# Moving the operands of a matmul stream to other SBUF addresses: a layernorm + S4 convolution + LoRA feed-forward kernel

## The chip, the cores and the metric

The kernel runs on one core of one Trainium2 chip, in one launch. The metric is the device time of an execution in microseconds (us). Before the change it is 442.14 us, the median of three executions (441.92 to 442.59).

## What is computed

x has 2048 rows of 512 channels. With xn the layernorm of each row:

```
s = causal convolution of xn along its 512 channels with an S4 kernel K, plus D * xn
ffn(xn) = W2' (silu(W1' xn) * (W3' xn))   hidden width 1376, each W' = W + 2 * B A (LoRA, rank 16)
out = x + s * silu(ffn(xn))
```

K comes from the S4 parameters (64 states) by a Cauchy sum and an inverse transform of length 512. All inputs are float32.

## The kernel before

**Tiling.** The rows are worked on in four blocks of 512 rows. Channels lie on the 128 partitions, in four chunks c of 128; the 512 rows of a block are the free dimension of every large matmul. The hidden width is cut into 11 tiles j (ten of 128, the last of 96). For a tile, TensorE computes the gate product (w1, bank h1), the up product (w3, bank h3), and the down product (w2, banks f0 to f3) of the tile before it. At the end of a block the S4 convolution is ten 128-square products of a Toeplitz tile `tzs` with the rows.

**Precision.** Each operand is held as two parts, high and low, in the type fp32r. `three` (lines 776 to 780) issues three matmuls for a product: low stationary with high moving (line 778), high with low (779), high with high (780). Each is a load of the stationary operand (LDWEIGHTS, 128 columns of 4 bytes) and a MATMUL that streams 512 columns of 4 bytes. So a gate, an up and a down product of one tile are 12 matmuls each, called a run below, and a block is 33 runs and 30 matmuls of convolution, 426 in all.

**Order.** The instructions are placed by hand. The block loop on TensorE is, for each tile, gate (12), up (12), down of the tile before (12); the last down tile alternates with the convolution, chunks 3 to 0. ScalarE does silu and the high part of the product, VectorE the multiplication and the low part; the normalized rows of the next block are made beside. The first block also folds the LoRA product into each weight tile as it comes from memory (small matmuls of lines 760 and 765 into two spare banks, then line 611, 493 and 621), and works out the S4 kernel on GpSimd. From then on the weights stay in SBUF.

**The layout.** Every partition holds the same byte map. `put` places a tensor at the next multiple of 32 bytes. Before the change the map starts with w13 (the folded w1 and w3), then w2f (the folded w2), xt (the split rows: two blocks, two parts, four chunks of 2048 bytes), the LoRA stack (over which `xres`, `gate` and others lie later), xn, g, ghl (the split product g: two parts of 2048 bytes), tz, tzs and small things. Scratch tensors of the first block lie inside regions that are filled later: `lora_first`, `lora_spread`, `lora_spread_split` and `rows_1` in w13, the S4 temporaries in w2f from tile 5, the raw weights in the second half of xt.

**Weight groups.** Tiles 0, 1 and 2 of w13 are groups by themselves; 3 and 4, 5 and 6, 7 and 8, 9 and 10 are pairs, kept by chunk, part and kind. A chunk of a single group is 512 bytes, of a pair 1024, of the last pair (128 + 96 columns) 896. `w13_tile` (line 331) gives the stationary operand of a product.

**Residues.** Taken modulo 2048 bytes and from the start of the map, in the kernel before: xt, all of w2f and the groups of w13 up to tile 8 start at 0, the up weights of the last pair at 1024, ghl and tzs at 128.

Of the kernel before, what the change touches and what calls it, by code (L numbers as in the profile page):

```python
# [28 lines left out]
F32R = mybir.dt.float32r  # L29

P = 128
D = 512
HID = 1376
R = 16
# [3 lines left out]
BLK = 512  # L38
NBLK = ROWS // BLK
RT = BLK // P  # L40
DC = D // P
HT = (HID + P - 1) // P
# [7 lines left out]
def hs(j):  # L50

    return min(P, HID - j * P)
# [7 lines left out]
def group(t):  # L60

    if t < PAIRED_FROM:
        return t, hs(t)
    t0 = t - (t - PAIRED_FROM) % 2
    return t0, hs(t0) + hs(t0 + 1)
# [7 lines left out]
def part_chunks(t):  # L73

    if t < PAIRED_FROM:
        return range(DC)
    h = t - group(t)[0]
    return range(h * DC // 2, (h + 1) * DC // 2)


def part_cols(t):
    return len(part_chunks(t)) * group(t)[1]


PART_AT = [sum(part_cols(u) for u in range(t)) for t in range(HT)]


# [8 lines left out]
LORA_FIRST = 3 * D + 5 * P  # L96
LANES_ST, LANES_MV = ST_COLS * R // P, MV_COLS * R // P
# [101 lines left out]
def build(nc, x, xT, w1, w3, w2, lora, lora_st, lora_mv, s4_lanes, s4_vc, s4_bp, s4_scalars, trig, lanes, dft, outT):  # L199
    ctx = ExitStack()  # L200
    with ctx:
        base = (nc.sbuf_base + 63) // 64 * 64

        def at(name, shape, off, dt=F32):
            return nc.alloc_sbuf_tensor_at(name, shape, dt, offset=base + off)


        top = [0]

        def put(name, shape, dt=F32):  # L210

            off = (top[0] + 31) // 32 * 32
            top[0] = off + int(np.prod(shape[1:])) * 4
            return at(name, shape, off, dt)

        w13 = put("w13", [P, 4 * DC * HID], F32R)
        w2f_off = top[0]
        w2f = put("w2f", [P, HT, 2, D], F32R)
        xt_off = top[0]
        xt = put("xt", [P, 2, 2, DC, BLK], F32R)  # L220
        lora_off = top[0]
        lst = put("lora_stack", [len(STACK) * R, LORA_COLS], F32R)
        xn_off = top[0]
        xn = put("xn", [P, RT, D])
        g = put("g", [P, BLK])
        ghl = put("ghl", [P, 2, BLK], F32R)
        tz = put("tz", [P, D])
        tzs = put("tzs", [P, 2, D], F32R)
        lane_c = put("lane_c", [P, EYE + P])
# [16 lines left out]

        raw = at("raw", [P, 6, BLK], xt_off + 2 * DC * BLK * 4)

        lr = at("lora_first", [R, LORA_FIRST], 7 * 4 * DC * P * 4)
        spread = at("lora_spread", [P, LANES_ST + LANES_MV], 4 * 4 * DC * P * 4)  # L250
        spread_hl = at("lora_spread_split", [P, 2, LANES_ST + LANES_MV], 5 * 4 * DC * P * 4, F32R)

        s4_tile = 5
        top[0] = w2f_off + s4_tile * 2 * D * 4
        trig_sb = put("trig_sb", [P, 2, D])
        den_re = put("den_re", [P, D])
        den_im = put("den_im", [P, D])
# [3 lines left out]
        even_odd = put("even_odd", [P, 2, D // 2])  # L261
        vc_sb = put("vc_sb", [NS, 2 * P])
        krow = put("krow", [P, P + D])
        assert top[0] <= w2f_off + HT * 2 * D * 4


        xres = at("xres", [P, 2, (xn_off - lora_off) // 4], lora_off)
        gate = at("gate", [P, 2, BLK], lora_off + DC * BLK * 4)
        rows_next = at("rows_next", [P, 2, D], lora_off + (DC + 2) * BLK * 4)
        scale_rows = at("scale_rows", [P, 2, BLK], lora_off + (DC + 4) * BLK * 4)  # L270
        assert lora_off + (DC + 6) * BLK * 4 <= xn_off

        rows_tile = 9
        rows_1 = at("rows_1", [P, RT, D], rows_tile * 4 * DC * P * 4)

        k_dram = nc.dram_tensor("k_scratch", [P, P + D], F32, kind="Internal")
        scales_dram = nc.dram_tensor("scales_scratch", [2, BLK], F32, kind="Internal")
# [2 lines left out]
        def bank(name):  # L280
            return ctx.enter_context(nc.psum_tensor(name, [P, BLK], F32))
# [3 lines left out]
        f = [bank(f"f{i}") for i in range(DC)]  # L285
# [45 lines left out]
        def w13_tile(kind, j, hl):  # L331

            t0, units = group(j)
            n = DC * units
            s = 4 * DC * P * t0 + ((kind // 2) * 2 + hl) * n
            u = (j - t0) * P
            return w13[:, s:s + n].rearrange("p (c u) -> p c u", c=DC)[:, :, u:u + hs(j)]

        def folded(kind, j, hl):

            if kind == 2:
                return w2f[0:hs(j), j, hl, :]
            t0, units = group(j)
            s = 4 * DC * P * t0 + ((kind // 2) * 2 + hl) * DC * units + part_chunks(j)[0] * units
            return w13[:, s:s + part_cols(j)]

        def raw_slot(kind, j):
# [2 lines left out]
        def raw_tile(kind, j):  # L350

            s = raw_slot(kind, j)
            return raw[0:hs(j), s, :] if kind == 2 else raw[:, s, 0:part_cols(j)]
# [10 lines left out]

        def resid(par, c):

            return xres[:, par, c * BLK:(c + 1) * BLK]

        def row_tile(b, r):

# [19 lines left out]
        def _(sync):  # L390
# [26 lines left out]
                sync.dma_start(raw_tile(kind, j), src).then_inc(raw_in[raw_slot(kind, j)], 16)  # L417

            def load_residual(b, par):
                dst = xres[:, par, 0:DC * BLK].rearrange("p (c r) -> p c r", c=DC)  # L420
                src = xT[:, :, bass.ds(b * BLK, BLK)]
                sync.dma_start(dst, src).then_inc(res0_in if isinstance(b, int) and b == 0 else res_in, 16)

            def store(b, par):
                for n, c in enumerate(OUT_ORDER):
                    sync.wait_ge(res_done, b * DC + n + 1)
                    sync.dma_start(outT[c * P:(c + 1) * P, bass.ds(b * BLK, BLK)], resid(par, c)).then_inc(out_done, 16)
# [60 lines left out]
        def _(act):  # L488
            def fold_hi(kind, j):
                act.wait_ge(fold_added, FOLD_NO[kind, j] + 1)  # L490
                if (kind, j) == (1, rows_tile):
                    act.wait_ge(stats_done, 2 * RT)
                nc.scalar.copy(folded(kind, j, 0), raw_tile(kind, j)).then_inc(whi_done, 1)  # L493
# [110 lines left out]
        def _(dve):  # L604
# [12 lines left out]
            def fold_lo(kind, j):  # L617
                if (kind, j) in POOL_LO:
                    return
                dve.wait_ge(whi_done, FOLD_NO[kind, j] + 1)  # L620
                nc.vector.tensor_tensor(folded(kind, j, 1), raw_tile(kind, j), folded(kind, j, 0).bitcast(F32),  # L621
                                        ALU.subtract).then_inc(wlo_done, 1)
# [42 lines left out]
            def out_sum(b, par):  # L665
                for n, c in enumerate(OUT_ORDER):
                    e = b * DC + n
                    dve.wait_ge(gate_done, e + 1)
                    dve.wait_ge(conv_ready, e + 1)
                    nc.vector.tensor_tensor(gate[:, n % 2, :], gate[:, n % 2, :], conv[c][:, :], ALU.mult) \  # L670
                        .then_inc(conv_used, 1)
                    dve.wait_ge(conv_used, e + 1)
                    if c < 2:
                        dve.sem_inc(spare_free[c], 1)
                    wait_residual(dve, b)
                    nc.vector.tensor_tensor(resid(par, c), resid(par, c), gate[:, n % 2, :], ALU.add) \
                        .then_inc(res_done, 1)
# [66 lines left out]
        def _(pe):  # L744
# [31 lines left out]
            def three(out, w, m, start, stop):  # L776

                pe.matmul(out, w[1], m[0], start=start, stop=False)  # L778
                pe.matmul(out, w[0], m[1], start=False, stop=False)  # L779
                return pe.matmul(out, w[0], m[0], start=False, stop=stop)  # L780

            def hidden(b, par, j, kind, out, rows=slice(0, BLK)):
                for c in range(DC):
                    if j == 0 and kind == 1 and not (isinstance(b, int) and b == 0):
                        pe.wait_ge(xlo_done, b * DC + c + 1)
                    mm = three(out[0:hs(j), rows], [w13_tile(kind, j, hl)[:, c, :] for hl in (0, 1)],
                               [xt[:, par, hl, c, rows] for hl in (0, 1)], c == 0, c == DC - 1)
                return mm
# [7 lines left out]
            def start():  # L796
# [16 lines left out]
                for c in range(DC):  # L813
                    pe.matmul(h1[:, lo], w13_tile(1, 0, 0)[:, c, :], xt[:, 0, 0, c, lo], start=(c == 0), stop=False)
                wait_split(pe, 1, 0)
                pe.wait_ge(xlo_done, RT // 2)
                for c in range(DC):
                    pe.matmul(h1[:, lo], w13_tile(1, 0, 1)[:, c, :], xt[:, 0, 0, c, lo], start=False, stop=False)
                    pe.matmul(h1[:, lo], w13_tile(1, 0, 0)[:, c, :], xt[:, 0, 1, c, lo], start=False, stop=(c == DC - 1))
# [21 lines left out]
                    pe.wait_ge(gate_done, b * DC)  # L841

            def down_chunk(j, c):
                return three(f[c][:, :], [w2f[0:hs(j), j, hl, c * P:(c + 1) * P] for hl in (0, 1)],
                             [ghl[0:hs(j), hl, :] for hl in (0, 1)], j == 0, j == HT - 1)

            def down(b, j):
# [88 lines left out]
        def _(pool):  # L936
# [28 lines left out]
            def next_scale(b, par):  # L965

                pool.wait_ge(scale_rows_in, 16 * b)
                pool.wait_ge(res_in, 16 * b)
                for c in range(DC):
                    tt(xnt[:, par, 1, c, :], resid(par, c), scale_rows[:, 0, :], ALU.mult).then_inc(scaled, 1)  # L970
# [5 lines left out]
            def fold_lo(kind, j):  # L976
                pool.wait_ge(whi_done, FOLD_NO[kind, j] + 1)
                tt(folded(kind, j, 1), raw_tile(kind, j), folded(kind, j, 0).bitcast(F32), ALU.subtract) \
                    .then_inc(wlo_pool, 1)
                pool.wait_ge(wlo_pool, POOL_LO.index((kind, j)) + 1)  # L980
# [157 lines left out]
```

## Time and profile before

| | |
|---|---|
| median of three executions | 442.14 us |
| span of the profiled execution | 439.7 us |
| TensorE matmul busy | 429.8 us, 98% of the span, 1868 matmuls |
| TensorE weight load busy | 341.6 us, 78% |
| VectorE, ScalarE, GpSimd busy | 159.6, 100.2, 63.6 us |
| DMA | 26.19 MB, mean 60 GB/s |

The span runs from the first to the last instruction of the profiled execution. Matmuls are pipelined: each is listed with about 0.39 us, but they start some 0.23 us apart, and it is the distance of the starts that makes the time. The matmul of the next product may have its stationary operand loaded while the one before streams (engine PEld beside PE).

### The profile page before, as it was taken

How to read it: one execution, taken by the hardware profiler on the slowest of the kernel's cores; microseconds unless marked ns; L12 is line 12 of the kernel's file. 1: busy time of each engine (PE TensorE's matmuls, PEld its weight loads, DVE VectorE, ACT ScalarE, POOL GpSimd, SP SyncE). 2: the span in 40 equal slices, each digit the busy share in tenths (PEclk: the TensorE clock that was granted, in tenths of full speed). 3: DMA queues.
4: the chain of work that ended last, by engine and by line, in shares of the span. 5: the costliest groups of instructions: out<-in, count | busy, mean ns of one | idle time of the engine just before them, and what ended most of it. 6: DMA issues, size and time to landing. Idle time of an engine off the chain costs nothing.

```text
span 439.7 us, 5019 instructions
## 1 busy us (share of the span) xinstructions
PE 429.8 (98%) x1868; PEld 341.6 (78%) x1868; DVE 159.6 (36%) x245; ACT 100.2 (23%) x167; POOL 63.6 (14%) x127
## 2 busy tenths in 40 slices
PE   8979999999999999999999999999999999999995
PEld 8857777776777888888878888888878888888774
DVE  3537665554539432122224232132224211111114
ACT  3433332232223111122112111122112111111111
POOL 1326541621222011400000011400000000000000
PEclk9989999999999999999999999999999999999998
DMA  8493643222040610100001510100002000000002
GB/s 267 114 197 104 220 144 97 66 70 75 18 133 37 215 49 0 48 1 0 1 0 72 167 48 0 48 0 0 0 0 86 10 0 0 0 0 0 0 0 95
DMA packets 14063, 26.19 MB, mean 60 GB/s; under 512 B 2480, under 2 KB 4208, under 8 KB 14032
## 3 DMA queue, kind: packets, MB, share of 16 engines
q1 hardware_dynamic: 13888, 25.41, 19.3%
q0 software_dynamic: 160, 0.59, 0.4%
q8 instruction: 8, 0.13, 0.1%
q14 instruction: 7, 0.06, 0.1%
HBM read 20.37 MB, written 4.53 MB: 57 GB/s over the span
## 4 chain that ended last, share of the span: by engine, by line
PE 92%; DMA 3%; SPq 1%; DVE 1%; ACT 1%; POOL 1%; issue 1%; DVEq 0%
PE h L778 20%; PE h L779 19%; PE h L780 19%; PE f L778 10%; PE f L780 9%; PE f L779 9%; DMA lora_stack<-lora_spread_split 2%; PE spare L765 2%; DMA xn<-x_dram 1%; PE spare L760 1%; SPq L457 1%; PE spare L780 1%; PE spare L778 1%; PE spare L779 1%; PE spare L884 0%
## 5 line engine op out<-in xcount | busy, mean ns | idle before, releaser
L778 PE MATMUL h<-xt,w 128*128 (+4 forms) x356 | 140.5, 395 | 0.6 <-DVE w L621 0.6
L779 PE MATMUL h<-xt,w 128*128 (+4 forms) x356 | 138.2, 388 | 0.0
L780 PE MATMUL h<-xt,w 128*128 (+4 forms) x356 | 138.1, 388 | 0.0
L778 PEld LDWEIGHTS h<-xt,w 128*128 128x128 f32 (+1 forms) x356 | 66.4, 186 | 18.4 <-issue 1.8
L657 DVE TENSOR_TENSOR g<-g,h 128x512 f32<-128x512 f32 (+1 forms) x44 | 30.2, 687 | 132.7 <-PE h L780 132.7
L780 PEld LDWEIGHTS h<-xt,w 128*128 128x128 f32 (+1 forms) x356 | 66.3, 186 | 15.0
L779 PEld LDWEIGHTS h<-xt,w 128*128 128x128 f32 (+1 forms) x356 | 66.3, 186 | 14.2
L662 DVE TENSOR_TENSOR ghl<-g,ghl 128x512 fp32r<-128x512 f32 (+1 forms) x44 | 32.7, 742 | 104.5 <-ACT ghl L519 104.4
L778 PE MATMUL f<-ghl,w2f 128*128 128x512 f32 (+1 forms) x176 | 70.3, 399 | 0.0
L780 PE MATMUL f<-ghl,w2f 128*128 128x512 f32 (+1 forms) x176 | 69.5, 395 | 0.0
L779 PE MATMUL f<-ghl,w2f 128*128 128x512 f32 (+1 forms) x176 | 69.2, 393 | 0.0
L519 ACT CAST ghl<-g 128x512 fp32r<-128x512 f32 (+1 forms) x44 | 27.3, 620 | 173.1 <-PE f L780 164.0
L778 PEld LDWEIGHTS f<-ghl,w2f 128*128 128x128 f32 (+1 forms) x176 | 33.0, 188 | 8.6 <-issue 0.3
L780 PEld LDWEIGHTS f<-ghl,w2f 128*128 128x128 f32 (+1 forms) x176 | 33.0, 188 | 7.8
L779 PEld LDWEIGHTS f<-ghl,w2f 128*128 128x128 f32 (+1 forms) x176 | 33.1, 188 | 7.5
L509 ACT ACTIVATE g<-h 128x512 f32<-128x512 f32 (+1 forms) x44 | 26.3, 598 | 54.2 <-PE h L780 53.8
L611 DVE SCALAR_TENSOR_TENSOR raw<-spare,raw 128x512 f32<-128x512 f32 (+2 forms) x33 | 22.3, 676 | 8.2 <-PE spare L765 7.1
L493 ACT CAST w<-raw 128x512 fp32r<-128x512 f32 (+1 forms) x22 | 13.4, 610 | 40.7 <-DVE raw L611 40.6
L949 POOL TENSOR_TENSOR scales<-moments,lane_c 128x2 f32<-128x2 f32 x8 | 2.3, 289 | 130.3 <-DVE moments L633 130.2
L949 POOL TENSOR_TENSOR normal_rows<-xres,scale_rows 128x512 f32 (+1 forms) x12 | 15.6, 1328 | 24.2 <-DMA scale_rows<-scales_scratch 12.2
L621 DVE TENSOR_TENSOR w<-raw,w 128x512 fp32r<-128x512 f32 (+1 forms) x18 | 14.4, 798 | 2.5 <-ACT w L493 2.4
L532 ACT ACTIVATE gate<-f 128x512 f32<-128x512 f32 x16 | 9.5, 598 | 22.2 <-PE f L780 19.6
(101 smaller groups left out, 270.8 us busy)
## 6 DMA issues: line engine op xcount, KB each, us to landing
raw<-w_dram SPq DMA_DIRECT2D x28, 256.0 KB, 3.4
xres<-xT_dram SPq DMA_DIRECT2D x4, 1024.0 KB, 7.2
outT_dram<-xres SPq DMA_DIRECT2D x16, 256.0 KB, 2.4
rows_next<-x_dram SPq DMA_DIRECT2D x4, 512.0 KB, 3.5
scale_rows<-scales_scratch SPq DMA_DIRECT2D x3, 512.0 KB, 3.8
xn<-x_dram SPq DMA_DIRECT2D x4, 256.0 KB, 4.3
rows<-x_dram SPq DMA_DIRECT2D x2, 512.0 KB, 7.1
raw<-w_dram SPq DMA_DIRECT2D x4, 224.0 KB, 2.5
```

Of the source, the lines that this page charges most:

```text
L493: nc.scalar.copy(folded(kind, j, 0), raw_tile(kind, j)).then_inc(whi_done, 1)
L509: nc.scalar.activation(g[0:hs(j), :], h1[0:hs(j), :], ACT.Silu).then_inc(silu_done, 1)
L519: nc.scalar.copy(ghl[0:hs(j), 0, :], g[0:hs(j), :]).then_inc(ghi_done, 1)
L532: nc.scalar.activation(gate[:, n % 2, :], f[c][:, :], ACT.Silu).then_inc(gate_done, 1)
L611: nc.vector.scalar_tensor_tensor(out=rt, in0=sp[bk][0:rt.shape[0], 0:fold_cols(kind, j)], scalar=LORA_SCALE, in1=rt, op0=ALU.mult, op1=ALU ...
L621: nc.vector.tensor_tensor(folded(kind, j, 1), raw_tile(kind, j), folded(kind, j, 0).bitcast(F32), ALU.subtract).then_inc(wlo_done, 1)
L657: nc.vector.tensor_tensor(g[0:hs(j), :], g[0:hs(j), :], h3[0:hs(j), :], ALU.mult).then_inc(g_done, 1)
L662: nc.vector.tensor_tensor(ghl[0:hs(j), 1, :], g[0:hs(j), :], ghl[0:hs(j), 0, :].bitcast(F32), ALU.subtract).then_inc(glo_done, 1)
L778: pe.matmul(out, w[1], m[0], start=start, stop=False)
L779: pe.matmul(out, w[0], m[1], start=False, stop=False)
L780: return pe.matmul(out, w[0], m[0], start=False, stop=stop)
L949: return nc.gpsimd.tensor_tensor(out, a, c, op)
```

## The change

The map is laid out anew; no instruction is added, removed or moved in the order of any engine.

- xt now comes first in the map (start 0), then w13, then w2f, then ghl, then the LoRA stack, xn, g and the rest.
- Each group of w13 is put at a residue modulo 2048 of its own, from a table: gate and up of tile 0 at 0 and 16, of tile 1 at 32 and 64, of tile 2 at 96 and 128, of pair 3 at 192 and 256, of pair 5 at 320 and 384, of pair 7 at 448 and 512, gate of pair 9 at 512, and its up weights right behind (1536).
- The down tiles, all in one tensor, get 0, 128, 256, 320, 384, 416, 448, 464, 480, 496 and 512 bytes of padding added up in front of them. With w2f at residue 512 their starts are at 512, 640, 768, 832, 896, 928, 960, 976, 992, 1008 and 1024; ghl behind them starts at 1024. tzs starts at 1152.
- The scratch tensors of the first block move with the tile that they lay in before. `xres` is addressed as one flat row with a computed start instead of a dimension for the two slots; the bytes are the same.

```diff
+STAGGER = {(1, 0): 0, (3, 0): 16, (1, 1): 32, (3, 1): 64, (1, 2): 96, (3, 2): 128, (1, 3): 192, (3, 3): 256,
+           (1, 5): 320, (3, 5): 384, (1, 7): 448, (3, 7): 512, (1, 9): 512}
+STAGGER_DOWN = (0, 128, 256, 320, 384, 416, 448, 464, 480, 496, 512)
+LINE = 2048
+def w13_starts():
+    at, top = {}, 0
+    for t0 in sorted({group(t)[0] for t in range(HT)}):
+        for kind in (1, 3):
+            at[kind, t0] = top if (kind, t0) == (3, 9) else top + (STAGGER[kind, t0] - top) % LINE
+            top = at[kind, t0] + 2 * DC * group(t0)[1] * 4
+    return at, top
...
-        w13 = put("w13", [P, 4 * DC * HID], F32R)
-        w2f_off = top[0]
-        w2f = put("w2f", [P, HT, 2, D], F32R)
         xt_off = top[0]
         xt = put("xt", [P, 2, 2, DC, BLK], F32R)
+        w13_off = top[0]
+        w13 = put("w13", [P, W13_BYTES // 4], F32R)
+        w2f_off = top[0]
+        w2f_at = [w2f_off + j * 2 * D * 4 + STAGGER_DOWN[j] for j in range(HT)]
+        w2f_all = put("w2f", [P, (w2f_at[HT - 1] - w2f_off) // 4 + 2 * D], F32R)
+        w2f = [w2f_all[:, (a - w2f_off) // 4:(a - w2f_off) // 4 + 2 * D].rearrange("p (h d) -> p h d", h=2) for a in w2f_at]
+        ghl = put("ghl", [P, 2, BLK], F32R)
         lora_off = top[0]
...
-        ghl = put("ghl", [P, 2, BLK], F32R)
...
             t0, units = group(j)
             n = DC * units
-            s = 4 * DC * P * t0 + ((kind // 2) * 2 + hl) * n
+            s = W13_AT[kind, t0] // 4 + hl * n
...
         def resid(par, c):
-            return xres[:, par, c * BLK:(c + 1) * BLK]
+            s = par * ((xn_off - lora_off) // 4) + c * BLK
+            return xres[:, bass.ds(s, BLK)]
```

## Rows read from the trace of the kernel before

**Rows 1.** The page: busy time of the engines, and the granted TensorE clock in 40 slices.
```profile
PE 429.8 (98%) x1868; PEld 341.6 (78%) x1868; DVE 159.6 (36%) x245; ACT 100.2 (23%) x167; POOL 63.6 (14%) x127
PEclk9989999999999999999999999999999999999998
```
**Rows 2.** The waits of TensorE, in total; then VectorE's multiplication, from the costliest groups.
```profile
PE spare L765 <- DMA lora_stack<-lora_spread_split: 2.9, 1, 2.9
PE h L794 <- DVE g L717: 1.1, 1, 1.1
...
L657 DVE TENSOR_TENSOR g<-g,h 128x512 f32<-128x512 f32 (+1 forms) x44 | 30.2, 687 | 132.7 <-PE h L780 132.7
```
**Rows 3.** Busy time in stretches: first block, the three others, the end.
```profile
core 0: us, PE busy (x) PEld busy (x) DVE busy (x) ACT busy (x) POOL busy (x), PEclk, DMA share, GB/s
0.00:140.90 140.90, 136.12 (x590) 103.69 (x591) 77.67 (x117) 46.83 (x79) 48.42 (x103) 0.99 0.42 118
140.90:238.75 97.85, 97.85 (x427) 79.37 (x426) 30.63 (x50) 19.28 (x32) 7.61 (x12) 1.00 0.12 41
238.75:336.60 97.85, 97.85 (x428) 79.37 (x426) 28.57 (x47) 18.20 (x31) 7.62 (x12) 1.00 0.12 38
...
434.44:439.80 5.36, 0.17 (x1) 0.00 (x0) 2.12 (x4) 0.11 (x1) 0.00 (x0) 0.70 0.32 122
```
**Rows 4.** TensorE's instructions in order of time, third block: first matmul of four runs.
```profile
249.63 0.40 PE L778 MATMUL f<-ghl,w2f 128*128 128x512 f32 x1
...
252.42 0.39 PE L778 MATMUL h<-xt,w 128*128 x1
...
255.16 0.39 PE L778 MATMUL h<-xt,w 128*128 x1
...
257.88 0.40 PE L778 MATMUL f<-ghl,w2f 128*128 128x512 f32 x1
```
**Rows 5.** The same view, tiles 9 and 10: first matmuls, some neighbours, the block's end.
```profile
310.15 0.39 PE L778 MATMUL h<-xt,w 128*128 x1
...
312.94 0.40 PE L778 MATMUL h<-xt,w 128*128 x1
...
313.41 0.39 PE L780 MATMUL h<-xt,w 128*128 x1
313.63 0.40 PE L778 MATMUL h<-xt,w 128*128 x1
313.87 0.39 PE L779 MATMUL h<-xt,w 128*128 x1
...
315.71 0.40 PE L778 MATMUL f<-ghl,w2f 128*128 128x512 f32 x1
...
318.50 0.40 PE L778 MATMUL h<-xt,w 128*96 x1
...
321.30 0.39 PE L778 MATMUL h<-xt,w 128*96 x1
...
324.07 0.39 PE L778 MATMUL f<-ghl,w2f 128*128 128x512 f32 x1
...
326.85 0.39 PE L778 MATMUL h<-xt,tzs 128*128 x1
...
336.60 0.39 PE L778 MATMUL h<-xt,w 128*128 x1
```
**Rows 6.** The same view, first block: gate, up and down runs between folding matmuls.
```profile
81.27 0.50 PE L778 MATMUL h<-xt,w 128*128 128x512 f32 x1
...
84.21 0.50 PE L765 MATMUL spare<-lora_stack 48*128 48x256 f32 x2
84.64 0.50 PE L778 MATMUL h<-xt,w 128*128 128x512 f32 x1
...
87.56 0.50 PE L765 MATMUL spare<-lora_stack 48*128 48x256 f32 x2
87.99 0.50 PE L778 MATMUL f<-ghl,w2f 128*128 128x512 f32 x1
...
90.97 0.49 PE L760 MATMUL spare<-lora_stack 48*128 48x512 f32 x1
```

More of the change, by code:

```diff
@@ L82, in part_cols @@
     return len(part_chunks(t)) * group(t)[1]
+STAGGER = {(1, 0): 0, (3, 0): 16, (1, 1): 32, (3, 1): 64, (1, 2): 96, (3, 2): 128, (1, 3): 192, (3, 3): 256,
[9 more added lines that the diff above has]
+    return at, top
+W13_AT, W13_BYTES = w13_starts()
 PART_AT = [sum(part_cols(u) for u in range(t)) for t in range(HT)]
@@ L247, in build @@
         raw = at("raw", [P, 6, BLK], xt_off + 2 * DC * BLK * 4)
-        lr = at("lora_first", [R, LORA_FIRST], 7 * 4 * DC * P * 4)
-        spread = at("lora_spread", [P, LANES_ST + LANES_MV], 4 * 4 * DC * P * 4)
-        spread_hl = at("lora_spread_split", [P, 2, LANES_ST + LANES_MV], 5 * 4 * DC * P * 4, F32R)
+        lr = at("lora_first", [R, LORA_FIRST], w13_off + W13_AT[1, 7])
+        spread = at("lora_spread", [P, LANES_ST + LANES_MV], w13_off + W13_AT[3, 3])
+        spread_hl = at("lora_spread_split", [P, 2, LANES_ST + LANES_MV], w13_off + W13_AT[1, 5], F32R)
         s4_tile = 5
-        top[0] = w2f_off + s4_tile * 2 * D * 4
+        top[0] = w2f_at[s4_tile]
         trig_sb = put("trig_sb", [P, 2, D])
@@ L263, in build @@
         krow = put("krow", [P, P + D])
-        assert top[0] <= w2f_off + HT * 2 * D * 4
-        xres = at("xres", [P, 2, (xn_off - lora_off) // 4], lora_off)
+        assert top[0] <= w2f_at[HT - 1] + 2 * D * 4
+        xres = at("xres", [P, (xn_off - lora_off) // 4 + DC * BLK], lora_off)
         gate = at("gate", [P, 2, BLK], lora_off + DC * BLK * 4)
@@ L273, in build @@
         rows_tile = 9
-        rows_1 = at("rows_1", [P, RT, D], rows_tile * 4 * DC * P * 4)
+        rows_1 = at("rows_1", [P, RT, D], w13_off + W13_AT[1, rows_tile])
         k_dram = nc.dram_tensor("k_scratch", [P, P + D], F32, kind="Internal")
@@ L341, in folded @@
             if kind == 2:
-                return w2f[0:hs(j), j, hl, :]
+                return w2f[j][0:hs(j), hl, :]
             t0, units = group(j)
-            s = 4 * DC * P * t0 + ((kind // 2) * 2 + hl) * DC * units + part_chunks(j)[0] * units
+            s = W13_AT[kind, t0] // 4 + hl * DC * units + part_chunks(j)[0] * units
             return w13[:, s:s + part_cols(j)]
@@ L419, in load_residual @@
             def load_residual(b, par):
-                dst = xres[:, par, 0:DC * BLK].rearrange("p (c r) -> p c r", c=DC)
+                dst = xres[:, bass.ds(par * ((xn_off - lora_off) // 4), DC * BLK)].rearrange("p (c r) -> p c r", c=DC)
                 src = xT[:, :, bass.ds(b * BLK, BLK)]
@@ L843, in down_chunk @@
             def down_chunk(j, c):
-                return three(f[c][:, :], [w2f[0:hs(j), j, hl, c * P:(c + 1) * P] for hl in (0, 1)],
+                return three(f[c][:, :], [w2f[j][0:hs(j), hl, c * P:(c + 1) * P] for hl in (0, 1)],
                              [ghl[0:hs(j), hl, :] for hl in (0, 1)], j == 0, j == HT - 1)
```

## The prediction

> **What bounds the kernel now.** I read the page first. TensorE is busy for 98% of the span, at a clock that is full in nearly every slice, and the other engines for at most 36% [rows 1]. Then its waits: the longest is 2.9 us, once, on a DMA in the first block, and VectorE for its part spends 132.7 us of idle time waiting for the up product [rows 2]. The stretches say the same with more force: blocks two to four take 97.85 us each with no idle time, at a granted clock of 1.00; only the first block (140.90 us, 136.12 busy) and the end (5.36 us) hold anything else [rows 3]. So the time is the number of matmuls times the distance of their starts, and nothing that an address change does to ScalarE, VectorE, GpSimd or a queue can show, except in those two places.
>
> The view that decides is therefore the order in time of TensorE's instructions, and in it the distance from the first matmul of a run of 12 to the first of the next. These distances are not all alike:
> - an up run of tile 2: 255.16 to 257.88, 2.72 us, 0.2267 us each; the gate run ahead of it, which follows a down run: 252.42 to 255.16, 2.74 (I use 2.735, as the rows are rounded) [rows 4];
> - a down run: 249.63 to 252.42, 2.79 us, 0.2325 each [rows 4]; another, 315.71 to 318.50, also 2.79 [rows 5];
> - gate and up of tile 9: 310.15 to 312.94 and on to 315.71, 2.79 and 2.77; of tile 10: 318.50, 321.30, 324.07, so 2.80 and 2.77 [rows 5].
>
> All these stream 512 columns at the same clock. Tile 9 writes the same banks with the same instructions as tile 2; what differs is where its operands lie. Take the offset of a product as the start of its stationary operand less that of its moving operand, modulo 512 bytes. In gate and up of tiles 0 to 8 it is 0. In the down runs it is -128 (ghl at 128, weights at 0). In tiles 9 and 10 the chunks are 896 bytes apart, so it walks through 0, 128, 256, 384. In the convolution it is 128 for all; the last stretch, 326.85 to 336.60, is 30 of those and the 12 of the last down tile, 9.75 us or 0.232 each [rows 5]. So every run whose products all have offset 0 takes 2.72 to 2.74 us, and every other 2.77 to 2.80.
>
> **The change part by part.** Count the 33 runs of a block by their offset afterwards. Gate 0 stays at 0, and up 7 and up 8 come to 512, which is 0. Up 0 goes to 16, gate 1 to 32, up 1 to 64, gate 2 to 96, up 2 to 128, gates 3 and 4 to 192, ups 3 and 4 to 256, gates 5 and 6 to 320, ups 5 and 6 to 384, gates 7 and 8 to 448: 15 runs leave offset 0. The down tiles, against ghl at 1024, come to 0, 128, 256, 320, 384, 416, 448, 464, 480, 496 and 0: two reach offset 0, nine stay off it. Tiles 9 and 10 and the convolution keep their offsets modulo 512.
>
> Price of a run off 0: the four of tiles 9 and 10 give 2.79, 2.77, 2.80, 2.77, the down runs 2.79; I take 2.785. No row has an offset that is not a multiple of 128. The bounds for these: single distances within the up run of tile 9 are as short as 0.22 us (313.41 to 313.63) and as long as 0.24 (to 313.87) [rows 5], so 12 of a kind would be 2.64 to 2.88; by whole runs the ends are 2.72 and 2.80. I take the run's mean, since the long and short distances follow one another in the same run.
>
> - Blocks two to four, each: seven of the 15 are gate runs behind a down run, 7 x (2.785 - 2.735) = 0.35; the other eight, 8 x (2.785 - 2.72) = 0.52. Gate 0, up 7 and up 8 stay aligned but now follow a run that isn't, 3 x 0.015 = 0.045. Down 0 and 10 gain 2 x (2.79 - 2.735) = 0.11. Net +0.80 us, three times: +2.4.
> - First block: the folding matmuls between the runs stretch all alike. A gate run there takes 81.27 to 84.21 = 2.94, an up run 84.64 to 87.56 = 2.92, a down run 87.99 to 90.97 = 2.98 [rows 6]; off 0 I take 2.98. Six ups (1 to 6) x 0.06 = 0.36, eight gates (1 to 8) x 0.04 = 0.32, down 0 and 10 give back 0.10. Net +0.6.
> - Rows first and ghl elsewhere, as absolute places: even and odd blocks use two halves of xt, 16 KB apart, and take 97.85 us both [rows 3]. I price the move at 0; it can cost or give only what the offsets do.
> - The other engines write and read the moved tensors. Their cover is the 132.7 us of idle time on VectorE [rows 2]; without cover, the end of the last block (5.36 us, four VectorE instructions in it [rows 3]) could move by some tenths. I take 0.
> - The scratch tensors lie in the same tiles and are filled in the same order; the 2.9 us wait on the stack's DMA [rows 2] stays, with some tenths either way as the bound. The flat `xres` has the same computed start; its register work lies on queues that wait for TensorE.
>
> Sum: 439.7 + 2.4 + 0.6 = 442.7 us of span. The median of the runs shown lies 2.4 above the span, so 445.1 us.
>
> The rule that speaks for another outcome is in the Trainium skill, "TensorE: Matmul & The Clock Gate", Part 2: TensorE has two independent read ports in SBUF, so loading the next weights takes no bandwidth from the running matmul; "SBUF — State Buffer" says under "Who interferes with whom" that TensorE waits on nobody. By it no address could matter. The trace doesn't agree: 0.2267 against 0.2325 us with nothing changed but the operands' places [rows 4, 5].
>
> **The rivals.**
> 1. Addresses don't matter; the 2.72 and 2.79 have another cause (the position behind a down run, the bank written). For it: gate runs behind a down run are slower than the up runs behind them. Against: tile 9's up run, which follows a gate run too, takes 2.77. Then all runs stay and the time is 442.1 us.
> 2. Several of the new offsets are as good as 0, and the down runs are the ones that win: faster. Mechanism: loading and streaming fall into step, as they visibly do at 0 (0.2267 without variation), and an offset of -128 happens to prevent it. The place is the nine down tiles with a new offset and the two at 0. If all runs with a uniform offset took 2.735, gates and ups would stand still and 11 down runs would give 0.055 each, 0.6 us per block: 2.4 us in all, 439.7 us. It decides from the share q of new offsets that lock: the 15 lose 0.87(1 - q) and the nine gain 0.50q with 0.07 gained anyway, so q must pass 0.58. Against it: 128, -128 and the mixtures all failed, and these are all we have.
> 3. Some offsets are much worse: small ones (16 to 96) where the two reads run through the same place together. If 15 gates and ups and nine downs went at 0.24 us a matmul, 2.88 a run: 15 x 0.15 + 9 x 0.09 = 3.1 us a block, 12 in all, 454 us; if only the five runs at 16 to 96 and the three downs nearest to 0 (464 to 496) do, 0.5 us a block more than forecast, 447 us.
>
> **How the numbers follow.** Forecast 0.52 (its own range 443.4 to 446.6), rival 1 0.13, rival 2 0.23, rival 3 0.12, most of it at its small form. The point is the forecast's, 445.1. The range is 439.8 to 447.6: it takes in most of rival 2 and the small form of rival 3, and leaves out all new offsets better than 0 and most of them at 0.24. Within 0.2% is 441.3 to 443.0, about what a measurement can tell from no change: rival 1 and a half-locked mixture, 0.16. Faster 0.22, slower 0.62.
>
> **What would show it.** In the profile after, the same view: blocks two to four at 98.6 to 98.7 us instead of 97.85; gate 0, up 7 and up 8 at 2.72 to 2.735 us; the gates and ups between at 2.77 to 2.80; down 0 at 2.72 to 2.74; tiles 9, 10 and the convolution as before; no new wait on TensorE. Wrong would be the forecast if runs at offsets such as 64 or 192 take 2.72 (rival 2), if all take what they took (rival 1), if some pass 2.82 (rival 3), or if down 0, now at offset 0, still takes 2.79: then the offset is not what counts.

## The result

In six runs each the changed kernel takes 444.34 us (443.33 to 444.94) against 442.36 (441.41 to 442.80) before: a ratio of 1.0049, 95% interval 1.0034 to 1.0065. It is slower by 0.5%. The forecast was 445.1 us, slower by 0.7%, range 439.8 to 447.6.

Read the page after first: the engines' busy times, and the clock in 40 slices, as in [rows 1].

```profile
PE 432.3 (98%) x1868; PEld 342.9 (77%) x1868; DVE 159.1 (36%) x245; ACT 100.3 (23%) x167; POOL 63.2 (14%) x127
PEclk9988999999999999999999999999999999999999
```

The same 1868 matmuls with 2.5 us more busy time, and nothing of note on the other engines. Next the stretches, cut at the first matmul of each block, with the columns of [rows 3].

```profile
0.00:142.44 142.44, 137.00 (x591) 104.46 (x591) 77.23 (x117) 46.88 (x79) 47.98 (x103) 0.98 0.43 117
142.44:240.83 98.39, 98.39 (x427) 79.54 (x426) 30.57 (x50) 19.34 (x32) 7.61 (x12) 1.00 0.13 41
240.83:339.22 98.39, 98.39 (x427) 79.53 (x426) 28.59 (x47) 18.25 (x31) 7.61 (x12) 1.00 0.11 37
339.22:437.60 98.38, 98.38 (x427) 79.34 (x425) 20.59 (x31) 15.77 (x27) 0.00 (x0) 1.00 0.03 12
437.60:443.00 5.40, 0.18 (x1) 0.00 (x0) 2.12 (x4) 0.11 (x1) 0.00 (x0) 0.99 0.31 121
```

A steady block takes 98.39 us where it took 97.85 [rows 3]: 0.54 us three times, 1.6 in all, still without idle time and at the full clock. The end is the same. The first block is 1.5 us longer in this profile; that is not the layout, as e8_again shows below.

Where the 0.54 us lie is to be read from TensorE's instructions in order of time, first matmul of each run of the third block (compare [rows 4]). The distance to the next row shown is the length of a run of 12.

```profile
240.83 0.39 PE L801 MATMUL h<-xt,w 128*128 x1
...
243.56 0.39 PE L801 MATMUL h<-xt,w 128*128 x1
...
246.29 0.39 PE L801 MATMUL h<-xt,w 128*128 x1
...
249.08 0.40 PE L801 MATMUL h<-xt,w 128*128 x1
...
251.88 0.39 PE L801 MATMUL f<-ghl,w2f 128*128 128x512 f32 x1
...
254.63 0.39 PE L801 MATMUL h<-xt,w 128*128 x1
...
257.44 0.39 PE L801 MATMUL h<-xt,w 128*128 x1
...
260.23 0.39 PE L801 MATMUL f<-ghl,w2f 128*128 128x512 f32 x1
...
263.01 0.39 PE L801 MATMUL h<-xt,w 128*128 x1
...
265.78 0.39 PE L801 MATMUL h<-xt,w 128*128 x1
...
268.51 0.39 PE L801 MATMUL f<-ghl,w2f 128*128 128x512 f32 x1
...
271.23 0.39 PE L801 MATMUL h<-xt,w 128*128 x1
...
273.98 0.39 PE L801 MATMUL h<-xt,w 128*128 x1
...
276.70 0.40 PE L801 MATMUL f<-ghl,w2f 128*128 128x512 f32 x1
...
279.50 0.40 PE L801 MATMUL h<-xt,w 128*128 x1
```

Gate 0 (offset 0) and up 0 (offset 16) take 2.73. Gate 1 and up 1, at 32 and 64, take 2.79 and 2.80 where they took 2.72; gate 2 and up 2, at 96 and 128, 2.81 and 2.79. But up 3 and up 4, at 256, take 2.73 and 2.72, and down 2, at 256, takes 2.72 (268.51 to 271.23), below every down run of before (2.79 [rows 4]). Gates 3 and 4, at 192, take 2.77 and 2.75. So the price is not one number for every offset but 0, and it repeats after 256 bytes.

### The profile page after: what moved, and what is told of

It reads as the page before. It is cut to its first block, busy times and chain, and to the rows that moved or that the text cites. A ratio compares the mean times of both kernels' runs of the same rounds, so it can differ in the third digit from the quotient of the medians.

```text
span 442.9 us, 5019 instructions
## 1 busy us (share of the span) xinstructions
PE 432.3 (98%) x1868; PEld 342.9 (77%) x1868; DVE 159.1 (36%) x245; ACT 100.3 (23%) x167; POOL 63.2 (14%) x127
## 4 chain that ended last, share of the span: by engine, by line
PE 94%; DMA 3%; SPq 1%; ACT 1%; DVE 0%; POOL 0%; issue 0%; DVEq 0%
PE h L801 20%; PE h L803 19%; PE h L802 19%; PE f L801 9%; PE f L802 9%; PE f L803 9%; PE spare L788 3%; DMA lora_stack<-lora_spread_split 2%; PE spare L783 1%; DMA lora_first<-lora_dram 1%; SPq L480 1%; PE spare L801 1%; PE spare L803 1%; PE spare L802 1%; PE f L796 0%; PE spare L907 0%
## 5 line engine op out<-in xcount | busy, mean ns | idle before, releaser
L801 PE MATMUL h<-xt,w 128*128 (+4 forms) x356 | 142.0, 399 | 0.0
L803 PE MATMUL h<-xt,w 128*128 (+4 forms) x356 | 139.7, 392 | 0.0
L802 PE MATMUL h<-xt,w 128*128 (+4 forms) x356 | 139.5, 392 | 0.0
L685 DVE TENSOR_TENSOR ghl<-g,ghl 128x512 fp32r<-128x512 f32 (+1 forms) x44 | 31.2, 708 | 104.2 <-ACT ghl L542 104.1
```

Source lines behind the costliest of these rows:

```text
L685: nc.vector.tensor_tensor(ghl[0:hs(j), 1, :], g[0:hs(j), :], ghl[0:hs(j), 0, :].bitcast(F32), ALU.subtract).then_inc(glo_done, 1)
```

## The experiments

**e1_ghl.** The layout of before; ghl lies right behind xt. (`xres` is addressed flat, as in the changed kernel.)

```diff
         xt = put("xt", [P, 2, 2, DC, BLK], F32R)
+        ghl = put("ghl", [P, 2, BLK], F32R)
...
-        ghl = put("ghl", [P, 2, BLK], F32R)
```

> The layout of before with one thing changed: ghl lies right behind xt, at residue 0 instead of 128, so that the down products have offset 0 against their weights. Theory (the offset of stationary to moving operand, modulo a small power of two, sets the distance): down runs go from 2.79 to 2.72 to 2.735 us, the gate runs behind them from 2.735 to 2.72, a steady block from 97.85 to about 97.1, the kernel 2.5 to 3 us faster (0.6%). Rival (the down runs are slow because of the bank they write or the operand they stream, not for their address): 97.85 stays, and so does the time.

Measured: 440.67 us, ratio 0.9960 (0.9946 to 0.9974). The stretch of the third block, and one down run:

```profile
239.35:336.48 97.13, 97.13 (x428) 79.36 (x426) 28.66 (x47) 18.21 (x31) 7.64 (x12) 1.00 0.12 38
```
```profile
250.24 0.39 PE L779 MATMUL f<-ghl,w2f 128*128 128x512 f32 x1
...
252.96 0.39 PE L779 MATMUL h<-xt,w 128*128 x1
```

The down run takes 2.72 us instead of 2.79, writing the same banks from the same weights. Of the operands of a steady block nothing but ghl has moved; the LoRA stack, xn and g, which lay between its old place and its new one, lie 4096 bytes higher. The theory holds; its gain, 1.7 us between the medians (442.37 and 440.67), is smaller than the 2.5 to 3 expected, though the blocks are at 97.13 as expected: three times 0.72 us are only 2.2.

**e2_order.** The changed kernel with both tables of padding at 0.

```diff
-STAGGER = {(1, 0): 0, (3, 0): 16, (1, 1): 32, (3, 1): 64, ...}
-STAGGER_DOWN = (0, 128, 256, 320, 384, 416, 448, 464, 480, 496, 512)
+STAGGER = {(1, 0): 0, (3, 0): 0, (1, 1): 0, (3, 1): 0, ...}
+STAGGER_DOWN = (0,) * 11
```

> The changed kernel with every padding of the two tables set to 0: xt first, ghl behind the down weights, all groups at residue 0 but the up weights of the last pair. Theory: absolute places count for nothing, so blocks take what they take in e1_ghl, about 97.1 us. Rival (the order of the map, rows first, costs or gains by itself): the blocks differ from e1_ghl's by more than 0.1 us.

Measured: 439.98 us, ratio 0.9950 (0.9938 to 0.9962). The second and third block:

```profile
141.45:238.58 97.13, 97.13 (x428) 79.37 (x427) 30.66 (x50) 19.30 (x32) 7.57 (x12) 1.00 0.13 41
238.58:335.71 97.13, 97.13 (x428) 79.35 (x426) 28.66 (x47) 18.18 (x31) 7.59 (x12) 1.00 0.12 38
```

97.13 us as in e1_ghl: the order of the map is worth nothing by itself. This splits the change in two. Its new order, by way of ghl at residue 0, is worth -0.72 us a block; its padding +1.26 (98.39 - 97.13).

**e3_aligned.** On top of e2_order, the chunks of the last pair padded to 1024 bytes, and tzs right behind ghl.

```diff
-            top = at[kind, t0] + 2 * DC * group(t0)[1] * 4
+            top = at[kind, t0] + 2 * DC * stride(t0) * 4
...
         ghl = put("ghl", [P, 2, BLK], F32R)
+        tzs = put("tzs", [P, 2, D], F32R)
```

(`stride` is 128 columns for tiles 0 to 2 and 256 for the pairs.)

> e2_order with the last pair's chunks padded from 896 to 1024 bytes and tzs put behind ghl at residue 0, so that all 426 products of a block have offset 0. Theory: every run takes 2.72 us or less, a block 426 x 0.2267 = 96.6 us, the kernel some 5 us (1.1%) faster than before. If the 32 array cycles that a matmul of 512 columns takes beyond 512 (0.2267 us x 2.4 GHz = 544) are one for each 16 bytes of stationary operand, the 96-column runs of tile 10 take 536 cycles a matmul, 2.68 us. Rival (tiles 9, 10 and the convolution are slow for another reason than the offset): they stay at 2.77 to 2.80 and the time is that of e2_order.

Measured: 439.14 us, ratio 0.9933 (0.9919 to 0.9947). The third block, then gate and up of tile 10:

```profile
238.25:335.00 96.75, 96.75 (x427) 79.33 (x426) 28.68 (x47) 18.21 (x31) 7.62 (x12) 1.00 0.12 38
```
```profile
317.14 0.39 PE L809 MATMUL h<-xt,w 128*96 x1
...
319.90 0.39 PE L809 MATMUL h<-xt,w 128*96 x1
...
322.67 0.39 PE L809 MATMUL f<-ghl,w2f 128*128 128x512 f32 x1
```

Tile 9 went from 2.79 and 2.77 to 2.72 and 2.72, the 12 matmuls of convolution 3 from 2.78 to 2.72. The guess on tile 10 is refuted: 2.76 and 2.77 us, not 2.68, although its offset is 0. A smaller stationary operand is not faster; its matmuls no longer keep the 0.2267 us of the others.

**e4_probe.** e2_order with other paddings of w13.

```diff
+STAGGER = {(1, 0): 4, (3, 0): 8, (1, 1): 24, (3, 1): 48, (1, 2): 80, (3, 2): 112, (1, 3): 144, (3, 3): 160,
+           (1, 5): 176, (3, 5): 208, (1, 7): 224, (3, 7): 240, (1, 9): 256}
```

> A map of new offsets in one run: e2_order with the gate and up weights at residues 4, 8 (tile 0), 24, 48 (1), 80, 112 (2), 144, 160 (pair 3), 176, 208 (pair 5), 224, 240 (pair 7) and 256 (gate of pair 9); the down products stay at offset 0. Theory (the period is 256 bytes and small distances from it, to either side, are good): 4 and 8 at 2.72 to 2.74, 240 at 2.75, 224 at 2.79, 24, 48, 80, 112 and 144 at 2.78 to 2.81, 160 to 208 falling from 2.80 to 2.76. Rival (no pattern; the distance is decided by what run went ahead): values that don't fit the ones of the changed kernel at 16, 32, 64, 96, 128, 192. Block about 97.9 us.

Measured, in a single run: 443.42 us, the third block 98.28. From the same view, tile 3: gate at 144, up at 160, then the down run at 0; behind them up 8, at 240.

```profile
261.96 0.39 PE L802 MATMUL h<-xt,w 128*128 x1
...
264.69 0.39 PE L802 MATMUL h<-xt,w 128*128 x1
...
267.49 0.40 PE L802 MATMUL f<-ghl,w2f 128*128 128x512 f32 x1
...
270.25 0.39 PE L802 MATMUL h<-xt,w 128*128 x1
```
```profile
306.19 0.39 PE L802 MATMUL h<-xt,w 128*128 x1
...
308.91 0.39 PE L802 MATMUL f<-ghl,w2f 128*128 128x512 f32 x1
```

Gate 2.73, up 2.80, down 2.76, and up 8 2.72. Runs of the third block by the offset modulo 256, worked out from the distances of first matmuls in both kernels and divided by 12 (ns):

```
offset mod 256    changed kernel (where)                          e4_probe
  0 (256, 512)    228 gate 0, 228 227 up 3 4, 228 227 up 7 8,
                  229 down 0, 227 down 2                          227 to 231 downs
  4, 8                                                            233, 231
 16, 24           227 up 0                                        231 (24)
 32, 48           233 gate 1                                      233 (48)
 64 (320)         233 up 1, 233 233 gate 5 6, 233 down 3
 80, 96           234 gate 2 (96)                                 232 (80)
112                                                               233
128 (384)         233 up 2, 233 233 up 5 6, 232 232 down 1 4
144                                                               228 228 gate 3 4
160 (416)         234 down 5                                      233 233 up 3 4
176                                                               230 230 gate 5 6
192 (448)         230 229 gate 3 4, 230 229 gate 7 8, 229 down 6
208, 224          232 (208) down 7, 233 (224) down 8              232 (208), 233 (224)
240               229 down 9                                      227 227 up 7 8
```

The two kernels agree where they meet (160, 208, 224; at 240 they differ by 2 ns), and in the changed one 64 agrees with 320, 128 with 384, 192 with 448, in gate, up and down runs alike. That speaks for a period of 256 bytes and against the rival. The shape was not as expected: 4, 8 and 24 are bad, 16 and 144 good. Down runs of e4_probe at offset 0 take up to 2.77 behind a disturbed run and 2.72 to 2.73 behind up 7 and up 8, at 240: settling costs several matmuls, so the run ahead counts too.

**e5_shift.** e3_aligned with the whole map moved up.

```diff
+        top[0] = 64
         xt_off = top[0]
```

> e3_aligned with 64 bytes put in front of the whole map: every operand lies 64 bytes higher, every offset between operands stays 0. Theory (only the distance between the two operands counts): runs of 2.72 us as in e3_aligned, blocks of 96.8 us. Rival (each operand's own residue counts, as when both have to start a line of 128 or 256 bytes): runs of 2.78 to 2.80, blocks near 98.5 us.

Measured: 438.16 us in a single run, blocks of 96.75 us.

```profile
237.58:334.33 96.75, 96.75 (x427) 79.33 (x426) 28.63 (x47) 18.18 (x31) 7.60 (x12) 1.00 0.11 38
```

Where both operands move together by 64 bytes nothing changes: at offset 0 it is the distance between them that counts, not the residue of either. At other offsets this was not tried.

**e6_full.** e3_aligned with tile 10 as a full tile, in 128 columns and 128 partitions; GpSimd and VectorE clear the unused weights once.

```diff
-            return ...[:, :, u:u + hs(j)]
+            return ...[:, :, u:u + P]
...
-                return three(f[c][:, :], [w2f[j][0:hs(j), hl, c * P:(c + 1) * P] for hl in (0, 1)],
-                             [ghl[0:hs(j), hl, :] for hl in (0, 1)], j == 0, j == HT - 1)
+                return three(f[c][:, :], [w2f[j][:, hl, c * P:(c + 1) * P] for hl in (0, 1)],
+                             [ghl[:, hl, :] for hl in (0, 1)], j == 0, j == HT - 1)
```

> e3_aligned with tile 10 treated as a full tile: 128 stationary columns in gate and up (32 of them zeros or not used), 128 partitions in down (the last 32 weights zero). More bytes, the same number of matmuls. Theory: equal loads fall into step as everywhere else, so the runs of tile 10, now 2.76 to 2.78 in e3_aligned, take 2.72, and the last down tile and the convolution 0.2267 us a matmul; a block goes from 96.75 to 96.6 us, the kernel 0.6 us faster than e3_aligned. Rival (a smaller load costs less and a larger one more): tile 10 gets slower or stays.

Measured: 438.33 us (437.83 to 439.52), ratio 0.9921 (0.9898 to 0.9945), the fastest version with a measured interval. Third block, and tile 10:

```profile
237.97:334.53 96.56, 96.56 (x428) 79.95 (x426) 28.57 (x47) 18.19 (x31) 7.59 (x12) 1.00 0.11 38
```
```profile
316.85 0.39 PE L819 MATMUL h<-xt,w 128*128 x1
...
319.57 0.39 PE L819 MATMUL h<-xt,w 128*128 x1
...
322.29 0.39 PE L819 MATMUL f<-ghl,w2f 128*128 128x512 f32 x1
```

Multiplying by 32 columns of nothing makes gate and up of tile 10 faster, 2.72 instead of 2.76. The down products of tile 10, with 96 of 128 partitions and all 128 columns, win by being filled too. Now every run takes 2.72, and the block is 426 x 0.22667 = 96.56 us to the last digit. The gain over e3_aligned is 0.19 us a block; the medians differ by 0.8 us, but their runs overlap (438.29 to 440.06 and 437.83 to 439.52), so only the blocks show it.

**e7_narrow.** The changed kernel with less to load in chunks 1 and 2.

```diff
+                    cols = slice(0, 32) if c in (1, 2) and not first_of else slice(0, hs(j))
-                    mm = three(out[0:hs(j), rows], [w13_tile(kind, j, hl)[:, c, :] for hl in (0, 1)],
+                    mm = three(out[cols, rows], [w13_tile(kind, j, hl)[:, c, cols] for hl in (0, 1)],
```

> The changed kernel, with chunks 1 and 2 of gate and up in blocks two to four multiplied for 32 of the 128 columns only (so three quarters of these two chunks are left out of the hidden product): six matmuls in a row load 32 columns instead of 128. Theory (the distance beyond 512 array cycles, 0.2133 us, is what the load of the next stationary operand takes from the stream, and the offset decides how much): among the narrow ones 0.216 to 0.220 us whatever the offset. Rival (the load is not what matters, the stream itself is slower for some addresses): the narrow ones keep their 0.227 to 0.234.

Measured, in a single run: 445.12 us, blocks of 98.63 us, 0.24 more than with full loads. The narrow matmuls are 0.224 to 0.242 us apart, 0.2316 on average over the third block, where the same matmuls with full loads have 0.2303. The expectation fell.

**e9_narrow_aligned and e10_narrow_after.** The same for whole runs, to leave no change of width within them, on e6_full and on the changed kernel. One matmul of 128 columns goes ahead of each run.

```diff
+                    cols = slice(0, P) if first_of or j == 0 else slice(0, 32)
+                    if c == 0 and not first_of and j > 0:
+                        pe.matmul(out[0:hs(j), rows], w13_tile(kind, j, 0)[:, 0, 0:hs(j)], xt[:, par, 0, 0, rows], start=True, stop=True)
```

> e6_full (all offsets 0), with gate and up of tiles 1 to 10 in blocks two to four multiplied for 32 of the 128 columns (the rest of the hidden product is left out), and one extra 128-column matmul ahead of each such run. So 12 matmuls in a row load 32 columns each and stream 512. In e7_narrow six of them in a row, between others, kept 0.226 to 0.238 us. Theory A (the stream of 512 columns itself takes 544 cycles, whatever is loaded beside it): 0.2267 us each. Theory B (the load takes it, and e7_narrow was only disturbed by the change of width): 0.215 to 0.220.

> The same edit on the changed kernel, with its offsets from 0 to 512 bytes: 12 matmuls in a row load 32 columns each. If the load is what disturbs the stream, a quarter of it disturbs a quarter as much: the runs at 32 to 128 bytes, 0.233 us each with 128 columns, come to 0.228 or below, nearer to those at 0 and 256. If the start of the load is enough, whatever its length, they stay at 0.231 to 0.234.

Measured: 455.74 and 458.91 us in a single run each (each steady block has 20 matmuls more). The up run of tile 3 in e9_narrow_aligned, and the gate run of tile 1, offset 32, in e10_narrow_after, with a neighbour each:

```profile
269.71 0.39 PE L830 MATMUL h<-xt,w 128*128 x1
269.94 0.39 PE L819 MATMUL h<-xt,w 128*32 x1
...
272.71 0.40 PE L819 MATMUL f<-ghl,w2f 128*128 128x512 f32 x1
```
```profile
251.28 0.39 PE L801 MATMUL h<-xt,w 128*32 x1
...
254.13 0.39 PE L812 MATMUL h<-xt,w 128*128 x1
```

With offset 0 and 32 columns, 269.94 to 272.71: 0.231 us each, neither A (0.2267) nor B (0.215 to 0.220). With offset 32, 251.28 to 254.13: 0.2375, more than the 0.2327 of the same run with full loads. The other three runs at 32 to 128 bytes (up 1 at 64, gate 2 at 96, up 2 at 128) come to 0.2316, 0.2308 and 0.2311, a little less than their 0.2332, 0.2341 and 0.2328 with full loads, but none to the 0.228 that a quarter of the disturbance would give. All other narrow runs of e10_narrow_after lie between 0.230 and 0.2325, those at offsets 0 and 256 too. Averaged over the 20 narrow runs of the third block the distance is 0.2313 us in e9_narrow_aligned and 0.2314 in e10_narrow_after: with 32 columns the offsets no longer make a difference on average, and a narrow load costs some 2% against a full one at offset 0.

**e8_again.** The changed kernel, a second profile.

> The changed kernel once more, for a second profile. Blocks two to four 98.39 us again. If the 1.5 us that the first block took longer in the first profile (142.44 against 140.90) are chance (the clock was at half for 6.8 us there and for 3.4 before the change), it may come out at 141.1 to 141.3; if the layout makes them, at 142.4.

Measured: 443.31 us, and these stretches; the last is the changed kernel's first profile at the same place.

```profile
0.00:141.04 141.04, 136.07 (x590) 103.63 (x591) 77.89 (x117) 46.89 (x79) 48.49 (x103) 0.99 0.43 118
239.45:337.85 98.40, 98.40 (x428) 79.43 (x427) 28.67 (x47) 18.26 (x31) 7.61 (x12) 1.00 0.11 37
33.00:36.00 3.00, 3.00 (x14) 2.18 (x13) 0.66 (x2) 1.21 (x2) 1.63 (x2) 0.86 0.05 21
```
```profile
33.00:36.00 3.00, 3.00 (x9) 2.24 (x7) 0.00 (x0) 1.42 (x3) 1.42 (x2) 0.50 0.02 8
```

The blocks repeat to 0.02 us. The first block takes 141.04 us, not 142.44: between 33 and 36 us the granted clock was 0.86 of full (14 matmuls) here and 0.50, the lower level of 1.2 GHz, there (9 matmuls). Ahead of it TensorE waits for the LoRA stack, 3.6 us in both profiles (2.9 before the change [rows 2]). Two executions of one kernel differ in how long the clock stays low; what decides it is not shown.

## Why the prediction was right, and where it was not

The reading of what bounds the kernel held: the time is the number of matmuls times the distance of their starts, and in the steady blocks no wait, queue or other engine entered it. That the distance depends on the offset between the operands, read from two groups of rows, is shown by e1_ghl (one operand moved, its runs from 2.79 to 2.72), e2_order (the map in another order, but the offsets of e1_ghl: the same block to 0.01 us) and e5_shift (everything moved, no offset, no effect). Rival 1, that addresses don't matter, is refuted by them.

The terms of the sum for a steady block, forecast +0.80, measured +0.54:

- The 15 runs that leave offset 0 cost 0.66 us, forecast 0.87. The step that failed is the one price of 2.785 for every offset but 0. It held for eight of them (2.79 to 2.81, at 32 to 128 and 320 to 384), but the four gates at 192 and 448 take 2.75 to 2.77, the two ups at 256 2.72 to 2.73, and the one at 16 2.73. The offsets in the rows of before were multiples of 128 taken modulo 512, and with a period of 256 the -128 of the down runs and the 128 of the convolution were one offset, not two. Modulo 256 the trace of before knew two values, and I counted four.
- Gate 0, up 7 and up 8 cost 0.04, forecast 0.045.
- Down 0 to 9 gain 0.20 us, where 0.11 was forecast for 0 and 10 together. Down 0, now at offset 0, takes 2.75, not 2.735, since it follows a disturbed run (behind a run at offset 0 it takes 2.72, in e1_ghl); the surprise is down 2, at 256, which gains 0.07 of it alone, with 0.05 for down 6 and 0.03 for down 9. Some new offsets are as good as 0, as rival 2 had it, but too few: put into its formula, the 0.66 us of the 15 runs give a share q of 0.24, and the 0.16 us that the nine down runs with a new offset gain give 0.32, where 0.58 decides.
- Tiles 9 and 10, the last down tile and the convolution together cost 0.05; the forecast had no change but the 0.055 that down 10 was to gain.
- Rival 3 did not occur: the longest run is gate 2's 2.81, and small offsets are no worse than middle ones. Its small form was also added up wrongly: four runs, not five, lie at 16 to 96, and with the three downs nearest to 0 at 2.88 they would cost 0.65 us a block, not 0.5.

The first block was forecast at +0.6. Between profiles with the same clock (at 1.2 GHz for 3.4 us in both) it is 141.04 against 140.90 [rows 3], so +0.1. The price of the runs is there all the same. The first and the seventh down run, before the change and in e8_again:

```profile
36.20 0.50 PE L778 MATMUL f<-ghl,w2f 128*128 128x512 f32 x1
...
99.78 0.50 PE L778 MATMUL f<-ghl,w2f 128*128 128x512 f32 x1
```
```profile
36.05 0.50 PE L801 MATMUL f<-ghl,w2f 128*128 128x512 f32 x1
...
100.10 0.51 PE L801 MATMUL f<-ghl,w2f 128*128 128x512 f32 x1
```

That is 63.58 us against 64.05, so +0.47, and the changed kernel's first profile has 64.05 too. What hid it is that e8_again reaches the first down run 0.15 us earlier and takes 0.19 us less from the seventh to the end of the block; how much of either the layout makes is not shown.

With 3 x 0.54 the sum is 1.8 us, and the medians differ by 1.98. So the direction and what bounds the kernel were right, and the size, forecast at 3.0 us, was half as much again too high: the steady blocks came to 98.39 us, not to the 98.6 to 98.7 that the prediction named as its sign, and down 0 to 2.75, not 2.72 to 2.74. That 445.1 is within 0.2% of 444.34 owes much to the smallness of the whole effect. The Trainium skill's rule of two independent read ports ("TensorE: Matmul & The Clock Gate", Part 2) would have put the difference at 0; the runs disagree, with 2.79 against 2.72 us for one run of 12 in e1_ghl.

What stays open is why. e7_narrow, e9_narrow_aligned and e10_narrow_after speak against the simplest account, that the load takes its share of the stream's reads in proportion to its columns: with a quarter of the columns no whole run is shorter than 0.230 us. The shortest distance held over a whole run in all these kernels is 0.2267 us, 544 cycles at 2.4 GHz for 512 columns. It was seen only at offset 0 or a few others, and with stationary operands of 128 columns: 12 equal loads in a row of 96 columns (e3_aligned) take 0.230, of 32 columns (e9_narrow_aligned) 0.231. Which part of the hardware has this rhythm was not shown.

## What to carry to other kernels

Where TensorE never idles, look at the distance between matmuls by run, not at its busy share: here it differed by 2.6% between runs of the same instructions. Put stationary and moving operand of one product at the same residue modulo 256 bytes, chunk strides included, and round an odd last tile up to the others' width; of 18 other residues tried in this kernel none was better than 0, and 16 and 240 came close. A table of different paddings gives each run another distance and the average of them, which was worse than no padding.

## What was not expected of the hardware

- The offset between the two operands of a matmul stream is worth some 3%: 0.2267 us at 0 and 256, 0.234 at 96, for 128 x 128 by 128 x 512 products in fp32r. It repeats after 256 bytes, and moving both operands together by 64 bytes at offset 0 changes nothing (e5_shift).
- 96 stationary columns cost more than 128 in such a stream (0.230 against 0.2267 us), and so do 32, with 0.231 to 0.232 at offset 0.
- The run ahead matters: at offset 0, the first three matmuls after a down run take 0.231 to 0.233 us before the rhythm sets in ([rows 4], 2.74 instead of 2.72). Behind other offsets it is up to eight, so that a run of 12 has a mean of 0.229 to 0.231 (down 0 to 5 of e4_probe). At one offset the run ahead can decide too: down 1, at 128, takes 0.2317 a matmul in the changed kernel and 0.2333 in e7_narrow, where the gate and up runs ahead have narrow loads.
- The same kernel's first block took 141.0 or 142.4 us, and the clock was at 1.2 GHz around the wait on the LoRA stack for 3.4 us in the one and 6.8 in the other.
